# A block of a macaron transformer on one core: the two feed-forward blocks change places, and k, the gram products and the first block are issued elsewhere

## The reference

```
x = x + 0.5 * ffn(layernorm(x))            # feed-forward: 256 -> 1024, exact gelu, -> 256
x = x + attn(layernorm(x))
x = x + 0.5 * ffn(layernorm(x))            # the same weights again
```

```
q, k, v = silu(conv4(x @ Wq)), silu(conv4(x @ Wk)), silu(conv4(x @ Wv))   # causal, per channel
beta = sigmoid(x @ Wb)                                       # one per token and head (4 heads, 64 wide)
q, k = l2norm(q), l2norm(k);  v, kb = v * beta, k * beta
A = -tril(kb @ k.T, -1)                                      # within a chunk of 32 tokens
Tm = inverse(I - A);  u = Tm @ v;  w = Tm @ kb
for each chunk:                                              # the recurrence, state S of 64 x 64
    u_i = u - w @ S;  o_i = q @ S + tril(q @ k.T) @ u_i;  S += k.T @ u_i
branches = [fir3(v), fir31(v), o, v]
w = softmax(gelu([x, mean/rms/max of branches, branches] @ gW1 + gb1) @ gW2 + gb2, with temperature and floor)
o = sum_i w_i * branch_i;  return rmsnorm(o) * onorm_w @ Wo
```

## Time and profile before

| | us |
|---|---|
| median of two runs | 1224.95 (1223.7 and 1226.2) |
| the profiled execution's own time | 1227.37 |
| its span (first to last instruction) | 1225.7 |
| PE busy | 1056.4 (86% of the span) |
| DVE busy | 820.9 (67%) |
| ACT busy | 549.3 (45%) |
| POOL busy | 415.6 (34%) |
| mean granted clock of PE | 0.932 of full speed |

### The profile page before, as it was taken

How to read it: one execution, slowest core, us unless ns; L and a number is a source line. 1 busy time by engine, 2 the same in 40 slices (tenths; PEclk the granted TensorE clock), 3 DMA queues, 4 the chain that set the end, 5 groups by cost and what they waited for, 6 DMA issues and landing times.

```text
span 1225.7 us, 25639 instructions
## 1 busy us (share of the span) xinstructions
PE 1056.4 (86%) x10348; PEld 784.7 (64%) x10348; DVE 820.9 (67%) x1556; ACT 549.3 (45%) x965; POOL 415.6 (34%) x648
## 2 busy tenths in 40 slices
PE   3778598899988999899988996999988998887838
PEld 2654485378745886488736884478736885477427
DVE  5774267785687767875788666875787667863263
ACT  1154236443374337543475336453475337532322
POOL 7106500671019500681028400681028400870000
PEclk9889699899999999989999999999999999995668
DMA  5040104110040203111040203011040204020000
GB/s 153 1 102 21 34 1 97 25 31 22 18 104 1 53 1 94 28 26 27 19 104 1 52 19 86 18 24 30 18 104 1 52 1 96 9 52 1 1 0 18
DMA packets 82293, 47.45 MB, mean 39 GB/s; under 512 B 57856, under 2 KB 75776, under 8 KB 82176
## 3 DMA queue, kind: packets, MB, share of 16 engines
q1 hardware_dynamic: 82176, 45.82, 16.4%
HBM read 31.12 MB, written 14.68 MB: 37 GB/s over the span
## 4 chain that ended last, share of the span: by engine, by line
PE 57%; DVE 22%; ACT 8%; issue 5%; SPq 3%; POOL 3%; DMA 1%; DVEq 0%; ACTq 0%; POOLq 0%
PE psum L782 12%; PE psum L784 10%; PE psum L783 10%; DVE conv_acc L1363 4%; PE psum L813 4%; DVE arena L1594 3%; PE psum L975 3%; PE psum L960 3%; PE psum L994 2%; PE psum L999 2%; SPq L347 2%; PE psum L1152 2%; ACT arena L582 2%; DVE arena L1596 2%; POOL arena L522 1%
## 5 line engine op out<-in xcount | busy, mean ns | idle before, releaser
L518 POOL TENSOR_TENSOR l_prod<-arena 64x30 f32<-64x30 f32 (+14 forms) x240 | 150.8, 628 | 599.2 <-DMA arena<-l_dram 581.0
L578 ACT ACTIVATE h_f<-psum,b_col 128x512 f32<-128x512 f32 x128 | 88.0, 688 | 216.4 <-PE psum L784 206.4
L522 POOL TENSOR_TENSOR arena<-arena,l_prod 64x30 f32<-64x30 f32 (+14 forms) x240 | 157.3, 655 | 18.8
L782 PE MATMUL psum<-w_hi,h_hi 128*128 128x256 f32 x512 | 152.0, 297 | 9.2 <-DVE h_lo L1343 9.2
L784 PE MATMUL psum<-w_hi,h_lo 128*128 128x256 f32 x512 | 145.2, 284 | 0.0
L783 PE MATMUL psum<-w_lo,h_hi 128*128 128x256 f32 x512 | 145.1, 283 | 0.0
L1081 PE MATMUL psum<-v_shift,fir_w 128*32 128x512 f32 x1152 | 133.6, 604 | 3.6 <-DMA v_shift<-v_dram 3.6
L1363 DVE SCALAR_TENSOR_TENSOR conv_acc<-psum,conv_col,conv_acc 128x511 f32<-128x511 f32 x144 | 107.8, 748 | 33.5 <-ACT conv_acc L603 22.4
L782 PE MATMUL psum<-xt_hi,w_hi 128*128 128x512 f32 x256 | 109.4, 427 | 14.3 <-DVE b_half L1456 7.0
L1342 DVE CAST h_hi<-h_f 128x512 fp32r<-128x512 f32 x128 | 65.3, 510 | 76.6 <-ACT h_f L578 40.1
L782 PEld LDWEIGHTS psum<-w_hi,h_hi 128*128 128x128 f32 x512 | 98.1, 192 | 15.3 <-DVE h_lo L1343 11.1
(11 more groups left out here) (232 smaller groups left out, 2205.6 us busy)
## 6 DMA issues: line engine op xcount, KB each, us to landing
x_in<-in_L_attn_x SPq DMA_DIRECT2D x8, 512.0 KB, 4.0
v_dram<-v_fm SPq DMA_DIRECT2D x8, 512.0 KB, 2.8
v_shift<-v_dram SPq DMA_DIRECT2D x8, 512.0 KB, 5.0
out<-x_tok SPq DMA_DIRECT2D x8, 512.0 KB, 2.9
v_shift<-v_dram SPq DMA_DIRECT2D x8, 511.0 KB, 7.0
v_shift<-v_dram SPq DMA_DIRECT2D x8, 510.0 KB, 9.1
v_shift<-v_dram SPq DMA_DIRECT2D x8, 509.0 KB, 11.6
arena<-in_L_ffn_w SPq DMA_DIRECT2D x2, 1024.0 KB, 7.1
```

Of the source, the lines that this page charges most:

```text
L518: pool.tensor_tensor(prod, l_inv[:, k + 1:, k:k + 1].broadcast_to(shape), l_inv[:, k:k + 1, 0:k].broadcast_to(shape), ALU.mult).then_inc(i ...
L522: pool.tensor_tensor(l_inv[:, k + 1:, 0:k], l_inv[:, k + 1:, 0:k], prod, ALU.add).then_inc(inverted, 1)
L578: act.activation(h_f[:, m % 2, :], bank, ACT.Gelu, bias=b1_col[:, m:m + 1]).then_inc(read, 1)
L782: pe.matmul(dst, a_hi, b_hi, start=first, stop=False, **kw)
```

## The change

The number of products, copies and transfers stays almost the same; their order changes, and with it the banks.

- The block that fills merge and recurrence is no longer the first block of sequence j but the second block of sequence i-1 (`upr`, `outr`). The first block is now that of sequence j+1 (`upw`, `outw`; `wide`), issued from after the q projections to before the mixture, in turn with the first half of the FIR slots. Three buffers `x_ring` hold a sequence's rows from load to store, in place of `x_in`, `x1_tok`, `x2_tok`; POOL's copy between them is gone.
- `ln2` of sequence j is turned in the last two tiles of the recurrence, and k's first half projected in the last tile. Then k's second half, beta, `k_t` and `k_products` come ahead of `gate_d` and of v.
- `beta` is computed tokens first: 24 matmuls with four columns moved, instead of six with 512, and `beta_turn` is gone.
- The passes are a head (which now holds the first block of sequences 0 and 1), `zero` (a pass with nothing to fill the recurrence with), five bodies, `last` (no first block left) and a tail (its recurrence is filled).
- SP stores and loads l before it sends v through DRAM; POOL adds the bias of sequence j+1 before the inversion.

The diff, cut to its core (of DVE and ACT the places where the order changes):

```diff
-        FFN_A = [("upa", (2, 3) + (2,) * (KT - 2)), ("outa", (3, 4))]
...
-        V = [("v", (1, 3))]
...
+        K = [("k", (2, 7)), ("beta", (0,))]
+        GATE = [("gate", (5, 6, 3, 4)), ("dv_t", (1, 0, 1, 0))]
+        GRAM = [("k_t", (2, 7)), ("gram", (0, 1))]
+        V = [("v", (2, 7))]
+        STAT = [("stat", (0,))]
+        Q = [("q", (1, 0)), ("hidden", (2,))]
+        LN1 = [("ln1", (7, 5))]
+        FFN_W = [("upw", (6, 5) * (KT // 2)), ("outw", (3, 4))]
...
             def fill(at, steps):
 
-                if at.front:
+                if at.fill:
                     for n in steps:
-                        ffn_step(at, 0, at.j, n)
+                        ffn_step(at, 0, at.i, n)
...
+                    if t == TILES - 1 and at.front:
+                        turn(at, "ln2", 1, lambda n: xn_tok[:, n, P:2 * P])
                     fill(at, range(10 + 6 * t + 2, 10 + 6 * t + 4))
...
                     fill(at, range(10 + 6 * t + 4, 10 + 6 * t + 6))
-                else:
-                    gate_f(at, 0)
-                    gate_f(at, 1)
+                elif at.front:
+                    copied(pe, at, "ln2", 0)
+                    copied(pe, at, "ln2", 1)
+                    projection(at, "k", 0, 0)
...
             def beta(at):
                 bank, full = claim(pe, at, "beta")
-                for k in range(HALVES):
-                    last = product3(pe, bank[0:32, :], wb_hi[:, k, :], wb_lo[:, k, :], xt_hi[:, k, :], xt_lo[:, k, :],
-                                    k == 0, k == HALVES - 1)
...
                 for t in range(TILES):
-                    last = pe.transpose(bank[:, 32 * t:32 * t + 32], beta_fm[:, P * t:P * t + P], ident[0:32, 0:32])
+                    toks = slice(P * t, P * t + P)
+                    for k in range(HALVES):
+                        last = product3(pe, bank[:, 32 * t:32 * t + HEADS], xt_hi[:, k, toks], xt_lo[:, k, toks],
+                                        wb_hi[:, k, 0:HEADS], wb_lo[:, k, 0:HEADS], k == 0, k == HALVES - 1)
                 last.then_inc(full, 1)
...
                 if at.front:
-                    turn_rows(at, "ln2", xn_made[1], j + 1)
+                    pe.wait_ge(silu_made, 6 * j + 2)
+                    to_tok(at, "k_t", lambda h: qk_fm[:, h, 0, :])
+                    k_products(at)
                 if at.back:
                     for h in range(HEADS):
                         copied(pe, at, "dv_t", h)
                         gate_d(at, h)
...
+                if at.ahead:
+                    turn_rows(at, "ln1", xn_made[0], j + 2)
+                    wide(range(0, 8))
...
+                if at.front:
+                    pe.wait_ge(v_shifted, 64 * j + 64)
+                    firs(at, 0, range(0, 2))
+                if at.ahead:
+                    wide(range(16, 20))
...
+                    firs(at, 0, range(8, 9))
+                    firs(at, 1, range(0, 2))
                 if at.back:
                     for b in range(2):
                         pe.wait_ge(norm_made, 2 * i + b + 1)
                         turn_tiles(at, "mix_t", b)
...
+                if at.front:
+                    k_rows()
+                if at.ahead:
+                    x_ready(dve, j + 1)
+                    stats(0, rows_of(j + 1))
+                if at.front:
+                    conv(2)
+                if at.ahead:
+                    normalise(0, j + 1, rows_of(j + 1))
                 if at.back:
                     copied(dve, at, "stat")
                     link(dve.tensor_scalar(stat_fm[0:D, :], stat_fm[0:D, :], 1e-4, None, ALU.max))
                     dve.sem_inc(stat_made, 1)
```

More of the change, by code:

```diff
@@ L191, in macaron_kernel @@
-        both = [MERGE, RECUR, FFN_A, STATS, LN2, V, STAT, K, LOGIT, FIR, Q, MIX, V_T, FFN_C, L_OFF]
-        ORDER = {"head": sum(front + [NEXT], first), "body": sum(both + [NEXT], []),
-                 "last": sum(both, []), "tail": sum(back, [])}
+        FFN_R = [("upr", (2, 3) + (2,) * (KT - 2)), ("outr", (3, 4))]
+        LN2 = [("ln2", (2, 7))]
+        K = [("k", (2, 7)), ("beta", (0,))]
+        GATE = [("gate", (5, 6, 3, 4)), ("dv_t", (1, 0, 1, 0))]
+        GRAM = [("k_t", (2, 7)), ("gram", (0, 1))]
@@ new lines, in macaron_kernel @@
+        LN3 = [("ln3", (7, 2))]
+        first = [("first", (2, 6)), ("upr", (2, 0) * (KT // 2)), ("outr", (3, 4)), ("sums", (5, 1))]
+        recur = [MERGE, RECUR]
+        early = [LN2, K, GATE, GRAM, V, STAT, Q]
+        ORDER = {"head": sum([LN2, K, GRAM, V, Q, LN1, FFN_W, FIR, V_T, L_OFF], first),
+                 "zero": sum(recur + early + [LN1, FFN_W, LOGIT, FIR, MIX, V_T, NEXT, L_OFF], []),
+                 "body": sum(recur + [FFN_R] + early + [LN1, FFN_W, LOGIT, FIR, MIX, V_T, NEXT, L_OFF], []),
+                 "last": sum(recur + [FFN_R] + early + [LOGIT, FIR, MIX, V_T, NEXT, L_OFF], []),
+                 "tail": sum(recur + [FFN_R, GATE, STAT, LOGIT, MIX, LN3, FFN_W], [])}
@@ L321, in macaron_kernel @@
         T_LOADS = CPT + 2 * (CPT - 1)
-        DVE_STEPS = {"head": 49, "body": 82, "last": 77, "tail": 38}
+        DVE_STEPS = {"head": 58, "zero": 71, "body": 81, "last": 66, "tail": 48}
         CONST_MADE, C_LOADED, SETUP_DVE = 60, 57, 36
@@ L691, in one_pass @@
-                    if not at.back:
-                        act.wait_ge(c_loaded, C_LOADED * 16)
-                    tap(0)
+                    out_of(at, "beta", 0, rows_tok[:, 1, :].rearrange("p (t h) -> p t h", t=TILES), ACT.Sigmoid,
+                           src=lambda b: b[:, 0:TILES * 32].rearrange("p (t h) -> p t h", t=TILES)[:, :, 0:HEADS])
+                if at.back:
+                    for h in range(2):
+                        out_of(at, "dv_t", h, dv_fm[h])
+                if at.front:
+                    silu(0)
+                    silu(1)
@@ L720, in one_pass @@
                 if at.front:
-                    for t in range(2):
-                        out_of(at, "k_t", t, arena[:, 0, 512 * t:512 * t + 512])
-                    out_of(at, "hidden", 0, hid_fm[:, :])
+                    wide_gelu(2)
+                    silu(4)
+                    silu(5)
                 if at.back:
@@ L1314, in normalise, with low @@
                     last.then_inc(xn_made[k], 1)
-                def low(k, seq, what):
-                    for h in range(HALVES):
+                def low(k, seq, what, ready=False, halves=range(HALVES)):
+                    for h in halves:
                         bank, read = arrive(dve, at, what, h)
@@ L1565, in one_pass @@
                 if at.front:
[L1566 to L1567 removed]
+                    conv(3)
                 if at.back:
[L1569 to L1570 removed]
+                    hidden(0)
+                    hidden(1)
+                if at.ahead:
+                    low(0, j + 1, "ln1")
+                if at.back:
+                    hidden(2)
+                    hidden(3)
                 if at.front:
[L1572 removed]
                     conv(4)
+                    wide_split(0)
                     conv(5)
+                    wide_split(1)
                 if at.back:
```

529 lines of the change are left out of this document (278 added, 251 removed).

## The result

The changed kernel takes 1257.45 us (median of two runs, 1256.3 and 1258.7) against 1224.95: the ratio is 1.0265, 95% interval 1.0204 to 1.0327. It is slower by more than 2%, outside the range (1187 to 1253) and 35 us above the forecast of 1222. The profiled execution took 1256.3 us, its span 1254.4.

The account below looks back on a forecast made before the run. PE's work was taken to bound a body: 127.3 us plus 11.7 of waits, 139.0, or 136.5 by placing, taken as 138. Pass changes summed to -3.2, giving 1224.2; the median, 2.4 lower, 1222 us, range 1187 to 1253.

Parts of the forecast that it names:

- the clock allowed for behind beta: In a body: nothing much for the clock; 0.3 us allowed after an idle 4 us, none for beta's matmuls.
- Net +0.7 us: PE's work in a body: new beta 2.5 us, less six old matmuls 1.4 and turn 0.4; range -1.8 to +1.1.
- the wait for the statistics: PE at the gate's statistics product: arrives at 620.5, `stat_made` at 624.6, so a new wait of 4.1 us.
- the middle between two sums: Body length: 139.0 us by adding work and waits, 136.5 by placing products one after another; middle 137.7, taken as 138.
- At k: PE at `k_t`, behind ACT's copies, table load and two silu: waits 2.0 us where it waited 1.3.
- at the first block's start: First block: begins 1.0 us late for its `xt_lo`, and its third "up" comes 2.0 us late.
- for splits: First block: three splits come 1.0 us late in all.
- for the strip pair: End of pass, no block left behind the attention products: PE waits 1.6 us for `lpair` to be read.
- Rival 1: Bodies: PE swallows the new waits, about 5 us idle left, 132.5 us a body; 1189 us, chance 0.26.
- Rival 2: Layer norm ahead of gate statistics: PE waits 8 us instead of 4, 1.5 for the clock; 1255 us, chance 0.17.
- Rival 3: Stretches without a cause come back in as many passes, at other places: 1236 us, chance 0.04.
- Rival 4: ACT pauses behind table loads on the road to k; `k_t` 2.8 us later in seven passes: 1241 us, chance 0.01.

Follow-up runs that it names:

- a_gated: Changed kernel with old beta, gate statistics before the layer norm, later strip-pair wait, and two of four `gate_d` products ahead of k's transposes: 1209.1 us, ratio 0.9856.
- a_lplate: Changed kernel with PE's wait for the last strip pair moved from the end of the pass to the merge that reads it: 1241.8 us, ratio 1.0133.

## Why the prediction was wrong

**The step that failed is the clock allowed for behind beta.** The prediction prices beta by its records alone ("Net +0.7 us") and adds for the clock "nothing much", 0.3 us behind the wait for the statistics. The records came as reckoned: the row takes 3.0 us (2.5 taken, 2.9 the upper end from transposes), the six old ones take 1.8 at this place (1.4 taken), the turn 0.4, net +0.8. But behind the row the granted clock falls to 0.64 and then 0.58, and that costs another 2.4 us in a body where it falls. PE is busy 130.5 in the mean body; 127.7 with the old beta. That is 2.8 us for beta where 0.7 stood. Over the run the new beta costs 15 us by itself and 19 with the two largest waits eased. The forecast had 0.7 in each of eight passes, 5.6 us, so 10 to 13 us of the miss of 35 are this term.

**The rest, by terms of the forecast.** The five bodies are 24 us over it, 4.8 each: 3.2 are PE's busy time (2.1 of them beta, 1.1 other: a body with the old beta was to have 126.6 and has 127.7), 0.6 the waits, 1.0 the middle between two sums, below. `zero` is 3.6 over, the head 2.1, `last` and tail 2.2, and 3.6 are that the median lies 1.2 above the profiled execution instead of 2.4 below. No single step carries this rest.

**The clock was argued from idle time only.** I allowed for a fall after an idle PE, from the row at 0.54. The trace of the changed kernel shows one behind a stretch that its records call 100% busy. The Trainium skill ("TensorE: Matmul & The Clock Gate", on LDWEIGHTS) has a weight load cost its columns / 1.2 ns; by that rule 24 loads are an estimated 2.6 us. The trace agrees: the starts are 0.11 us apart.

**The middle between two sums was wrong.** The waits and the work added to 139.0, the placing gave 136.5, and I took 138. A body's length is PE's busy time plus its idle time: the mean body has 130.5 + 12.3 = 142.8. What the placing took off for overlap did not come.

**The waits came near in their sum, less so one by one.** At k 1.80 (predicted 2.0); for the statistics 2.75 (4.1); at the first block's start 1.14 and 1.50 (1.0 and 2.0); for splits 2.25 (1.0); for the strip pair 2.30 (1.6); at the mixture none (none). Their sum in this body, with 0.44 us of small ones, is 12.2 against 11.7; that it is so close is in part luck, as 1.35 too much at the statistics stands against 1.25 too little at the splits. At the statistics both sides came later than placed: PE 64.6 us into the body instead of 61.5, `stat_made` 67.4 instead of 65.6. With the old beta PE arrives at 61.5, as placed, and the product starts at 64.2. So the chain behind `k_t` is itself 1.4 us shorter than reckoned, and the 3.2 us that the row and the clock cost pass on in full, through `k_t` and `k_rows`, to `stat_made`. The splits came late in the block that takes turns with FIR.

**Head, `zero`, `last`, tail.** `last` (122.8 for 122) and the tail (120.9 for 119.5) came as reckoned, the head's first merge waited 1.1 us for something else and not for the inverse, and the head took 151.1 for 149. `zero` was to be 4 us over a body and is 2.8 over. Its unfilled recurrence ran at half clock:

```profile
155.00:191.00 36.00, 29.43 (x206) 26.72 (x207) 14.82 (x39) 8.40 (x19) 0.00 (x0) 0.50 0.01 1
```

**The rivals.** Rival 1 did not happen; even a_gated, the fastest order, took 1209 against its 1189. Rival 2 gave nearly the right time, 1255, by the wrong road: its wait was to be 7.5 us or more, and it was 2.75 in this body and at most 3.1 in any. That a late `k_t` passes on undiminished to `stat_made`, as it says, did happen, and so did its "1.5 for the clock", at other waits and without them. Rival 3: behind the head of the changed kernel the longest stretch without a cause is 1.7 us; the old ones of 6.5 and 8.1 did not come back. Rival 4: none of the 12 table loads of this body has a pause behind it that another engine did not end; the silu of k starts 0.01 us behind the end of its load.

```profile
633.29 1.28 ACT L621 ACT_TABLE_LOAD   x1
634.58 1.15 ACT L621 ACTIVATE qk_fm<-conv_acc 128x512 f32<-128x512 f32 x2
```

**What stays open.** What else decides whether the clock falls behind the 24 matmuls: a_lplate shows both cases in bodies of one run, and why it falls at all no run here shows. Of the rest of the miss (22 to 26 us of 35) the edits show that 12 to 16 us can be had by moving one wait; that is what an order is worth, and not a step of the forecast that failed. The heads of the profiled executions lie between 150.3 and 157.8 us; I did not look into why.

## What to carry to other kernels

Price a row of matmuls that move few columns at the starts of its weight loads (here 0.11 us each), and then ask what the granted clock does behind it: in the records the row looks 100% busy. Such a row costs less where waits of other engines follow it. Where PE is busy 90% and each wait is 1 to 3 us, put something that is already there into the wait (two gate products ahead of k: -11 us), or move the other engine's step (statistics first: -12.5). Do not add up gains of edits that remove the same fall of the clock (-52 us one by one, -31 together). Small groups of another kind between dependent products hide the vector engine's splits; taking the turns away cost 40 us.

## What the hardware showed that I had not expected

- The granted clock fell to 0.64 behind 3.0 us of 24 four-column matmuls with no idle time at all. Right behind such a row it was low in 38 of 49 passes, right behind six wide matmuls in none of 42.
- With 48 of them the clock fell while the row still ran: the second 24 took 3.9 us instead of 3.0.
- Two bodies of one run, with the same instructions, lasted 140.5 and 143.7 us; one has a deeper fall at the same place and one more at its end.
- A recurrence with nothing between its steps ran at 0.50 for 36 us, though PE was busy in 29 of them.
